# Two more scan tiles with exponentials in PSUM, and a twelfth product on GpSimd, in a graph and state-space kernel

## What is computed

```python
dbc = u @ w_xp
dt = softplus(dbc[:, :DT_RANK] @ w_dt + b_dt)
B = dbc[:, DT_RANK:DT_RANK + D_STATE]
C = dbc[:, DT_RANK + D_STATE:]
dA = exp(dt[:, :, None] * A[None])
dBu = dt[:, :, None] * B[:, None, :] * u[:, :, None]
def step(hst, inp):
    dAt, dBut, Ct = inp
    hst = dAt * hst + dBut
    return (hst, hst @ Ct)
_, ys = scan(step, zeros, (dA, dBu, C))
```

## Time and profile before

| | |
|---|---|
| median of three runs | 1087.23 us |
| the profiled execution, its own time | 1086.18 us |
| its span, first to last instruction | 1084.6 us |
| VectorE busy | 995.6 us, 92% of the span |
| TensorE busy | 971.7 us, 90% |
| ScalarE busy | 559.5 us, 52% |
| GpSimd busy | 337.6 us, 31% |
| mean granted TensorE clock | 0.958 of full speed |
| first product with B in window 0 (VectorE) starts at | 516.8 us |
| the last window's at | 1012.7 us |

### The profile page before, as it was taken

The page is one execution under the profiler, slowest core; times in us unless marked ns, Lnnn a source line. Parts: engine busy times, 40 slices in busy tenths (PEclk is TensorE's granted clock), DMA queues, the critical chain, the costliest instruction groups (busy, mean ns, idle before and its releaser), DMA issues. The chain is left out here.

```text
span 1084.6 us, 13272 instructions
## 1 busy us (share of the span) xinstructions
PE 971.7 (90%) x4134; PEld 671.6 (62%) x4134; DVE 995.6 (92%) x735; ACT 559.5 (52%) x1110; POOL 337.6 (31%) x228
## 2 busy tenths in 40 slices
PE   2889999999999999999998998989989999877665
PEld 2667777777777777634554564655646556445554
DVE  5989999999999999771999999999999999999996
ACT  3343343434343434225583875767847758477342
POOL 5450202020202021100532634426335263253652
PEclk9899999999999999999999999999999999988566
DMA  9999999999999999963825535365164452211200
GB/s 255 259 267 312 332 310 347 324 345 321 355 324 343 324 341 343 225 213 140 309 98 212 213 103 195 142 215 213 61 223 165 175 179 83 97 68 68 99 1 20
DMA packets 190396, 233.72 MB, mean 215 GB/s; under 512 B 8880, under 2 KB 164592, under 8 KB 175760
## 3 DMA queue, kind: packets, MB, share of 16 engines
q1 hardware_dynamic: 105936, 163.60, 46.3%
q10 hardware_dynamic: 80896, 60.57, 20.8%
q0 software_dynamic: 3520, 9.04, 2.8%
HBM read 170.00 MB, written 63.18 MB: 215 GB/s over the span
## 5 line engine op out<-in xcount | busy, mean ns | idle before, releaser
L958 DVE STREAM_TRANSPOSE at<-rows 128x1024 f32<-128x1024 f32 x136 | 267.8, 2011 | 21.9 <-DMA rows<-in_adj 7.5
L546 POOL TENSOR_TENSOR dBuP<-dtu,b_sb 128x1024 f32<-128x1024 f32 x77 | 182.9, 2376 | 282.1 <-DVE dtu L1074 115.1
L1223 PE MATMUL yT<-ah,xh 128*128 128x512 f32 x512 | 212.3, 415 | 34.8 <-DVE al L966 27.0
L599 ACT ACTIVATE ah<-at 128x2048 fp32r<-128x2048 f32 x64 | 122.6, 1915 | 211.4 <-PE yT L1223 196.1
L1310 PE MATMUL bank<-adjc,xm 128*128 128x512 f32 x448 | 206.0, 595 | 0.8 <-ACT axT L680 0.8
L1223 PE MATMUL yT<-al,xh 128*128 128x512 f32 x512 | 202.1, 395 | 0.0
L1223 PE MATMUL yT<-ah,xl 128*128 128x512 f32 x512 | 201.9, 394 | 0.0
L1420 PE MATMUL yT<-ident,pr 128*128 128x128 f32 x1008 | 147.4, 294 | 37.7 <-DVE pr L1139 31.2
L1420 PEld LDWEIGHTS yT<-ident,pr 128*128 128x128 f32 x1008 | 128.1, 152 | 67.9 <-DVE pr L1139 45.6
L834 ACT ACTIVATE dA<-dt,A_sb 128x512 f32<-128x512 f32 x182 | 122.6, 711 | 43.0 <-DVE dt L1071 43.0
L1139 DVE TENSOR_TENSOR pr<-hs,bank 128x1024 f32<-128x1024 f32 x112 | 134.3, 1199 | 11.2 <-PE bank L1402 11.0
(11 more groups left out here) (187 smaller groups left out, 1190.0 us busy)
## 6 DMA issues: line engine op xcount, KB each, us to landing
adjT<-at SPq DMA_DIRECT2D x56, 1024.0 KB, 7.5
adjc<-adjT SPq DMA_DIRECT2D x56, 1024.0 KB, 5.3
rows<-in_adj SPq DMA_DIRECT2D x152, 256.0 KB, 8.3
rows<-in_adj ACTq DMA_DIRECT2D x136, 256.0 KB, 8.7
b_sb<-b_dram ACTq DMA_DIRECT2D x37, 512.0 KB, 4.9
xm<-in_x SPq DMA_DIRECT2D x4, 512.0 KB, 10.7
res<-in_x POOLq DMA_DIRECT2D x8, 256.0 KB, 7.1
mid<-xn POOLq DMA_DIRECT2D x8, 256.0 KB, 7.9
```

What stands on the lines that cost most here:

```text
L546: nc.gpsimd.tensor_tensor(dBu(n, par)[:, :, 1:], dtu[par][:, :, :], b_sb[load % 2][:, nB(n) % 2:nB(n) % 2 + 1, :].to_broadcast([P, H, TILE ...
L599: nc.scalar.activation(ah[c % 2][:, :], at[c % 2][:, :, :].rearrange("p m t -> p (m t)"), ACT.Copy)\
L958: last = nc.vector.transpose(dst.rearrange("p m (g i) -> p g m i", i=32), src.rearrange("p g (i m) -> p g m i", i=32))
L1223: last = mm(acc[k][:, :], w[:, b, :], v[c % 2][:, cols], start=(b == 0 and j == 0), stop=(b == KB - 1 and j == 2))
```

## The change

Six tables change, and three places that follow from them. Above them the lengths `NPB = len(POOL_B)` and `NVB = S - NPB` go from 11 and 5 to 12 and 4.

```diff
-POOL = (1, 2, 3, 4, 5, 6, 7, 9, 11, 13, 15)
-IN_BANK = (1, 2, 3, 4, 5, 6)
+POOL = (1, 2, 3, 4, 5, 6, 7, 8, 9, 11, 13, 15)
+IN_BANK = (1, 2, 3, 4, 5, 6, 7, 8)
 CARRIED = tuple(k for k in range(S) if k not in IN_BANK)
-B_LOADS = ((1, 2), (3, 4), (5, 6), (7, 9), (11, 13), (15,))
-B_LOAD_AT = {3: 2, 5: 3, 8: 4, 11: 5}
-POOL_AFTER = {n: 2 if n <= 7 else 3 for n in POOL}
+B_LOADS = ((1, 2), (3, 4), (5, 6), (7, 8), (9, 11), (13, 15))
+B_LOAD_AT = {3: 2, 5: 3, 6: 4, 10: 5}
+POOL_AFTER = {n: 2 if n <= 9 else 3 for n in POOL}
...
-                 6: [("B", 8), ("B", 10), ("C", 9), ("C", 10), ("B", 14), ("C", 13), ("C", 15)]}
+                 6: [("B", 10), ("C", 9), ("C", 10), ("B", 14), ("C", 13), ("C", 15)]}
...
-        dA_bank = {1: M1, 2: bank[6], 3: M1, 4: bank[6], 5: bank[6], 6: bank[6]}
+        dA_bank = {1: M1, 2: bank[6], 3: M1, 4: bank[6], 5: bank[6], 6: bank[6], 7: bank[6], 8: bank[6]}
...
-            return (dBuV[1], dBuP[1], dBuV[0], dBuP[0])[n % 4]
+            return (dBuV[0], dBuP[0], dBuV[1], dBuP[1])[n % 4]
...
-                        elif 4 <= n <= 6:
+                        elif 4 <= n <= 8:
                             act.wait_ge(half_scanned, len(IN_BANK) * b + (2 if n == 4 else n - 1))
...
-                if (kind, n) == ("B", 8):
+                if (kind, n) == ("B", 10):
                     pe.wait_ge(half_scanned, len(IN_BANK) * (b + 1))
```

## The result

The changed kernel takes 1085.57 us in the median of 20 runs, the kernel before, on the same chip, 1089.05 in the median of 20. The ratio is 0.997, with a 95% interval of 0.9957 to 0.9982: the change saves 0.3%, 2.0 to 4.7 us, where 5.6 were forecast. In the profiled executions it is 1084.07 us (span 1082.5) against 1086.18.

The account below looks back on a forecast made before the run. VectorE sets a window's length, TensorE close behind; each window gains the lesser saving, TensorE's. Windows 0 to 4 give 3.5 us, window 5 0.3, window 6 1.8: 5.6 off 1087.23, so 1081.6 us, range 1079.3 to 1085.6.

Parts of the forecast that it names:

- the binding chain: From state 7 to pr(7), VectorE's and TensorE's chains run side by side; a window gains the lesser saving, TensorE's.
- Windows 1 to 5: Windows 1 to 4 gain TensorE's waits for B(8) plus 0.50 us of matmul each; window 5 gains 0.3.
- window 0: First window, no tail: u ends half a us after z's old place, so 0.3 us off, bounds 0 and 0.7.
- window 6: TensorE's sum of state 4 can go 1.84 us sooner; 1.8 us taken, 1.0 or less if matmuls slow, at most 2.2.
- VectorE's part: Up to pr(7): 1.13 us saved on a product, some 0.1 lost on scans; 1.0 us a window.
- TensorE's part: Without B(8), a wait of 0.34 and a matmul of 0.50 go: C(7) comes 0.84 us sooner in window 3.
- ScalarE's part: Exponentials of state 8 wait for 7's first-half scan; table load 1.6 us late, u still 0.1 us ahead of z.
- GpSimd's part: One more 2.38 us product a window costs nothing; load for 9 and 11 costs zero, between 0 and 0.5 a window.
- the signs of being wrong: TensorE waits for u in windows 1 to 6; L1057 for L736; L1127 over 2 us; GpSimd for B in most windows.
- the second (u late for z in every window): u half a us late for z; no more than 0.3 of 0.84 us kept a window, 2.1 in all, 1085.1 us; chance 0.15.
- VectorE alone: TensorE catches up elsewhere, so each window gains VectorE's 1.0 us, window 6 some 2.2: 8.2 in all, 1079.0 us; chance 0.10.
- The collision with second-half scans: GpSimd's products stretch both new L1127 to 2.25 us; pr(7) 0.4 us later, 2.9 us slower, 1090.1 us; chance 0.04.

Follow-up runs that it names:

- the block moved: Changed kernel with one of three blocks of adj moved from TensorE's step 6 to step 11; ratio 0.9927 against the kernel before.
- the early rows: Changed kernel with the rows of B for 9 and 11 loaded at step 5 into a free scratch tile; ratio 0.9963 against the kernel before.
- the product-only kernel: Kernel before with the twelfth product on GpSimd, but states 7 and 8 still scanned in one piece; ratio 0.9996 against the kernel before.

## Why the prediction was right or wrong

The direction and the binding chain were right. The size was not: 5.6 us forecast, 3.5 measured. The steps that failed are terms of the sum, all too large. Windows 1 to 5 stood in it with 3.4 us and are worth some 2.5; window 0 with 0.4, and it lost 0.2; window 6 with 1.8, and it is worth some 0.9 at an equal clock.

- **VectorE's part: right.** It reached pr(7) at 763.80 - 0.36 = 763.44, 33.35 us after the start, with a second-half scan of state 8 of 1.50 us ahead of it, lengthened by the late product; forecast was 762.85 - 729.77 = 33.08. So the wait left there was 0.36 us, where some 0.6 was forecast. With the block moved, pr(7) stood at just 33.08, without a wait.
- **TensorE's part, 0.84 in window 3: right at C(7)**, which moved by 0.84, and wrong by a little behind z. The window gained 0.71, since z's second half meets u's second half (1.99 us instead of 1.89).
- **ScalarE's part: right in its numbers, wrong in what followed.** The margin of u against z was put at 0.1 us and was about 0. The forecast treated that as safe. The runs show that the change replaced one loop from VectorE to TensorE (through B(8)) by another of the same length (through the exponentials of 8 and u). The wait before sz fell to 0.64 us; 0.4 was forecast.
- **Windows 1 to 5 are the step that failed first.** The sum took TensorE's whole saving in each of windows 1 to 4 and 0.3 for window 5, because that one profile had the low clock in window 5 alone. Of ten such windows in two profiles, three had it before and five after, too few to say that the change makes it commoner. A window with it gains 0.26, which is the 0.3 taken for window 5, and one without it 0.67. With the low clock in four of ten in either kernel, as it was in the mean, windows 1 to 5 are worth 5 x (0.6 x 0.67 + 0.4 x 0.26) = 2.5 us. The sum held 3.4: waits of 0.36, 0.21, 0.34 and 0.21 us in windows 1 to 4, four matmuls of 0.50, and the 0.3.
- **Window 0: the forecast of 0.3 us lost was too small.** TensorE's saving there was 0.21 + 0.50 = 0.71 us, and the window became 0.2 us longer, so 0.9 us was lost, more than the bound of 0.7. z waited for u by 0.72 and 1.80 us. In the second profile VectorE then waited for C and for L736; in the first it ran back to back behind the scan of 2.97 us.
- **GpSimd's part, zero: right for the products, wrong for the load.** The load for 9 and 11, given 7.1 us to land, made GpSimd wait 2.97 us in window 0 of the first profile and 1.34 to 1.61 us in three later windows of the two. A wait for rows of B in most windows stood among the signs of being wrong, and it came, in five of seven. Yet it cost nothing that the length of windows 1 to 5 shows, since VectorE waits for C behind it. In window 0 the early rows and the second profile, both without that wait, were hardly shorter, or longer.
- **Window 6: the figure of 1.8 was met once, by luck, and its step failed.** The wait for B(8) went, and the sum of state 4 moved up by 1.15 and 1.75 us. But in the second execution TensorE's convolution ran at the low clock, 5.14 us instead of 4.39, and 0.75 us was left. The forecast had named this case and gave it too little. In the mean of the two it is 1.3; at an equal clock it is some 0.9.

Together, at an equal clock: 2.5 + 0.9 - 0.2 = 3.2 us, and 3.5 with the 0.3 of the last window, which the sum put at nothing. Measured are 3.5, with an interval of 2.0 to 4.7, so how well this agrees is in part luck. On the scale of the forecast, where the kernel before is 1087.23, the measured saving gives 1083.7 us: inside the range, 2.1 us above the forecast of 1081.6.

Of the rivals, the second (u late for z in every window) came nearest in its figure, 1085.1 us on a scale where before is 1087.23, but not in its mechanism: at full clock u cost some 0.1 us and not half a us. VectorE alone did not set the windows. The collision with second-half scans stayed small there; the mean of L1127 is 1473 ns. It was real where the change had not removed its target, in the long scans of the product-only kernel. The Trainium skill (SBUF — State Buffer, Who interferes with whom) calls the port pair a lock held for a whole instruction. The traces agree within 0.2 us: the scan of 3.58 us is 1.22 longer than one alone, with 1.43 us of the product left, and that of 3.78 us is 1.42 longer, with 1.63 left.

What stays open: why the clock is granted low in some windows and not in others with the same idle times before it. That the change makes it commoner is not borne out: it came in 9 of the 20 windows 1 to 5 in the four profiles of kernels with eleven products on GpSimd, and in 26 of 65 in the thirteen with twelve.

## What to carry to other kernels

When two engines' waits are nearly equal, removing one uncovers the other: compute the margin of the next chain, and count a margin of 0.1 us as a bound, not as cover. Two edits that do next to nothing alone can be worth 0.8 us a window together, so test them in pairs. And a sum built window by window from a single profile inherits that profile's luck with the clock; take a second profile of the kernel before first.

## What the runs showed that was not expected

- The granted clock at the start of a window, after TensorE had idled 1.24 and 1.17 us for pr, was 1.00 or, in the mean of 8 us, 0.82 to 0.87, by window and execution. A window of the kernel before then took 71.14 to 71.23 us instead of 70.14 to 70.18.
- With a block of adj moved away, the kernel before took 70.34 and 70.12 us in its two low-clock windows. So half a us less of TensorE's work ahead of C(7) hides the loss there.
- In the four profiles of the table, all eight of windows 1 to 5 with a star, and none of the other twelve, had GpSimd wait 2.1 to 2.5 us for the rows of B of state 7. VectorE was busy by no more than 0.2 us longer in them. Which of the two, if either, brings on the other is not shown.
- A scan of 2.35 us that started while GpSimd's product ran took 3.2 to 4.2 us in most windows, while first halves with exponentials in PSUM took 1275 ns in the mean of 56, against 1473 for the second halves in SBUF.
- In window 6 the same eight matmuls of the convolution took 3.60, 4.16, 4.39 and 5.14 us in the four executions. The clock granted meanwhile was 1.00 in the shortest case and 0.70 in the longest.
- Loads of 512 KB for two rows of B landed after 4.7 us in the median and 10.0 at most; a load's cover has to be read from the longest, not from the median.
